# Graph network of four layers on one core: the maximum's products in four row groups, the output projection in two banks

## What is computed

```python
# layer 0: normalised graph convolution, batch norm over all graphs, relu, + res_weight * h
# layer 1: attention over 8 heads of 32
scores = einsum('bhnd,bhmd->bhnm', Q, K) / sqrt(32)
attn = softmax(where(adj == 0, -inf, scores))
out = einsum('bhnm,bhmd->bhnd', attn, V) @ Wo.T + bo
# layer 2: (eps * x + adj @ x) @ W1 + b1, rms norm, silu, @ W2 + b2   (hidden width 1024)
# layer 3: attention of 4 heads with scores leaky_relu(e_i + e_j), masked, softmax, @ h
```

## Time and profile before

| | |
|---|---|
| median of 3 executions | 3992.91 us |
| lowest and highest | 3992.35 and 9107.89 us |
| profiled execution: span | 3982.8 us, the only time shown of it |
| PE busy | 3709.5 us (93%) |
| DVE busy | 3101.9 us (78%) |
| ACT, POOL busy | 1994.8 us (50%), 1576.2 us (40%) |
| mean granted TensorE clock | 0.953 |

### The profile page before, as it was taken

One profiled execution on the slowest core, in us unless ns is written; L12 is line 12 of the kernel. 1 busy time (PEld: TensorE's weight loads), 2 busy tenths in 40 slices (PEclk: granted clock), 3 DMA queues, 4 the chain that ended last, 5 costly groups with the idle time before them and its releaser, 6 DMA issues.

```text
span 3982.8 us, 59433 instructions
## 1 busy us (share of the span) xinstructions
PE 3709.5 (93%) x19042; PEld 2707.6 (68%) x19042; DVE 3101.9 (78%) x5637; ACT 1994.8 (50%) x3047; POOL 1576.2 (40%) x980
## 2 busy tenths in 40 slices
PE   7999579999999999999999999999999999999986
PEld 6888346676667766666666676766677666666665
DVE  6787557888887888888888888888878888888752
ACT  4656145555555555555545545555555555555430
POOL 4667234333443444444433333334434444444310
PEclk9999689999999999999999999999999999999986
DMA  8988322222222212222222222222222212222200
GB/s 286 317 310 298 93 53 64 70 69 69 63 58 69 60 52 56 53 69 69 69 69 69 69 69 69 69 69 63 58 69 59 58 52 53 69 69 69 53 16 11
DMA packets 195935, 341.10 MB, mean 86 GB/s; under 512 B 28720, under 2 KB 64432, under 8 KB 195888
## 3 DMA queue, kind: packets, MB, share of 16 engines
q1 hardware_dynamic: 195888, 340.50, 30.3%
HBM read 188.89 MB, written 50.33 MB: 60 GB/s over the span
## 4 chain that ended last, share of the span: by engine, by line
PE 78%; DVE 10%; ACT 4%; issue 3%; POOL 2%; DMA 2%; SPq 1%; DVEq 0%; ACTq 0%; POOLq 0%
PE bank L1444 12%; PE bank L1495 12%; PE obank L1378 12%; PE bank L1233 9%; PE pair L1233 7%; PE pair L1362 7%; PE bank L1406 6%; PE bank L1463 3%; PE pair L1339 3%; DVE minus_max L1033 2%; PE obank L1265 2%; DMA pT<-in_adjT 2%; PE bank L1265 1%; DVE b_st L841 1%; ACT hsq L632 1%
## 5 line engine op out<-in xcount | busy, mean ns | idle before, releaser
L602 POOL TENSOR_TENSOR pT<-pT,node_edge 128x1024 f32<-128x1024 f32 x256 | 628.6, 2462 | 532.0 <-ACT pT L690 530.1
L690 ACT ACTIVATE pT<-pair 128x1024 f32<-128x1024 f32 x512 | 515.9, 1031 | 325.6 <-PE obank L1378 248.2
L1033 DVE TENSOR_REDUCE minus_max<-pair 128x2 f32<-128x1024 f32 x512 | 603.3, 1216 | 56.9 <-PE pair L1339 56.5
L1023 DVE TENSOR_TENSOR pT<-pT,node_edge 128x1024 f32<-128x1024 f32 x256 | 399.8, 1562 | 269.4 <-ACT pT L690 266.2
L1495 PEld LDWEIGHTS bank<-v,p3T 128*128 128x128 f32 x4096 | 502.4, 199 | 36.2 <-DVE p3T L1182 24.5
L1495 PE MATMUL bank<-v,p3T 128*128 128x65 f32 x4096 | 499.8, 280 | 20.2 <-DVE p3T L1182 20.2
L540 POOL TENSOR_TENSOR d_rs<-d_ve,minus_half 128x4 f32<-128x4 f32 x32 | 32.2, 1007 | 1207.5 <-DVE d_ve L853 1207.5
L1378 PE MATMUL obank<-pT,v 128*64 128x512 f32 x2048 | 490.3, 611 | 8.4 <-POOL pT L602 4.8
L1444 PE MATMUL bank<-w_s,hid 128*128 128x256 f32 x2048 | 479.6, 389 | 0.3 <-DVE hid L1112 0.3
L1444 PEld LDWEIGHTS bank<-w_s,hid 128*128 128x128 f32 x2048 | 383.6, 192 | 87.7 <-issue 40.1
L632 ACT ACTIVATE p3T<-x,d_sh,d_rs 128x256 f32<-128x256 f32 x128 | 66.4, 589 | 720.6 <-POOL d_sh L546 720.6
(11 more groups left out here) (189 smaller groups left out, 6468.7 us busy)
## 6 DMA issues: line engine op xcount, KB each, us to landing
pT<-in_adjT SPq DMA_DIRECT2D x64, 512.0 KB, 5.3
a_at<-in_adjT SPq DMA_DIRECT2D x64, 512.0 KB, 3.6
q_parts<-high_parts SPq DMA_DIRECT2D x256, 128.0 KB, 4.7
k_parts<-high_parts SPq DMA_DIRECT2D x256, 128.0 KB, 4.1
b_at<-in_adjT SPq DMA_DIRECT2D x64, 512.0 KB, 3.9
hid<-in_x SPq DMA_DIRECT2D x32, 512.0 KB, 4.4
x_res<-hid SPq DMA_DIRECT2D x32, 512.0 KB, 5.0
pre_bn<-hsq SPq DMA_DIRECT2D x32, 512.0 KB, 4.1
```

What stands on the lines that cost most here:

```text
L602: nc.gpsimd.tensor_tensor(half, half, node_edge[:, 0:2, :], ALU.mult).then_inc(a_masked[0].sem, 1)
L690: nc.scalar.activation(dst, pair[p][:, :, :], func, **more).then_inc(a_copied[p].sem, 1)
L1023: nc.vector.tensor_tensor(half, half, node_edge[:, 2:4, :], ALU.mult).then_inc(a_masked[1].sem, 1)
L1033: nc.vector.tensor_reduce(minus_max[:, t, 2 * two_heads:2 * two_heads + 2], pair[p][:, :, :], AX.X, ALU.max, negate=True).then_inc(a_copie ...
```

## The change

- `a_nat` does two former steps at once: for one node block and four heads, four matmuls in four row groups (0, 32, 64, 96) into both pairs, after a wait for both. There are 8 such steps. They stand in `ORDER` where the first or the second of the two steps stood; `a_max` keeps its 16 steps and their places and follows the new layout.
- The output projection goes to `bank[0]` and `bank[1]` (V_WO); the waits of DVE, POOL and `b_ln` follow. The two banks have 8 fills a graph for 7.
- `minus_max` is wider, set to zero once, and is transposed with 128 columns.
- `put_shift` issues one DMA for 8.
- The sorting is split: the high parts wait for the high parts alone (and the last scores), the low parts for the low ones. Number and order of its DMAs stay.
- The remaining steps of `ORDER` keep their order. A scratch size of the builder is set to 1024.

The diff, cut to its core:

```diff
@@ -16,8 +16,8 @@
 A_FILLS = 18
-O_FILLS = 1 + H1 // 2 + 2
-B_FILLS = (7, 7, 6 + 2 * H3)
+O_FILLS = 1 + H1 // 2
+B_FILLS = (8, 8, 6 + 2 * H3)
 RING = 4
@@ -77,16 +77,15 @@
-b.sumsq4:2 b.tanh0:3 p.v1:0 h.values31:3 b.tanh1:3 a.load0:0 a.nat00:0 a.nat01:0 b.out20:2 a.nat10:0 a.headc3:2
-a.vmask1:1 p.qhigh:1 a.nat11:0 b.tanh2:3 b.out21:2 h.prob0:3 a.vmask2:1 h.head0:3 a.nat20:0 a.nat21:0 b.out22:2
...
-b.flip31:2 a.div0:1 b.diag:2 a.nat61:0 b.e:2 a.vmask6:1 a.nat70:0 b.sumsq7:2 b.scale0:2 b.scale1:2 a.vmask7:1
...
+b.sumsq4:2 b.tanh0:3 p.v1:0 h.values31:3 b.tanh1:3 a.load0:0 a.nat0:0 b.out20:2 a.nat1:0 a.headc3:2 a.vmask1:1
+p.qhigh:1 b.tanh2:3 b.out21:2 h.prob0:3 a.vmask2:1 h.head0:3 a.nat2:0 b.out22:2 a.nat3:0 a.vmask3:1 b.out23:2 a.wo0:1
+a.nat4:0 b.tanh3:3 p.khigh:1 h.prob1:3 a.wo1:1 a.vmask4:1 a.nat5:0 h.head1:3 p.vc:1 b.norm3:3 b.ms:2 a.vmask5:1
+b.flip30:2 b.sumsq5:2 a.nat6:0 h.prob2:3 b.sumsq6:2 b.flip31:2 a.div0:1 b.diag:2 b.e:2 a.vmask6:1 a.nat7:0 b.sumsq7:2
...
@@ -163,7 +162,7 @@
         node_edge = sb("node_edge", P, T, N, dt=bf16)
-        minus_max = sb("minus_max", P, T, H1)
+        minus_max = sb("minus_max", P, (T - 1) * H1 + P)
         row_buf = sb("row_buf", P, N)
@@ -279,10 +278,9 @@
         a_qk_in = signal("a_qk_in", 24, 16)
-        a_shift_in = signal("a_shift_in", H1, 16)
+        a_shift_in = signal("a_shift_in", 1, 16)
         a_filled = [signal(f"a_filled{i}", A_FILLS) for i in range(2)]
         a_copied = [signal(f"a_copied{i}", A_FILLS) for i in range(2)]
-        wo_sum = signal("wo_sum", 2)
         shift_sum = signal("shift_sum")
@@ -321,7 +319,7 @@
         U_HT, U_Q, U_K, U_V, U_NAT, U_ST = 0, 1, 2, 3, 4, 20
-        V_AGG, V_HID, V_MS, V_RB, V_OUT, V_HT, V_E, V_VT, V_V3, V_HEAD = 0, 2, 10, 11, 12, 14, 16, 17, 18, 20
+        V_WO, V_AGG, V_HID, V_MS, V_RB, V_OUT, V_HT, V_E, V_VT, V_V3, V_HEAD = 0, 2, 4, 12, 13, 14, 16, 18, 19, 20, 22
@@ -481,28 +479,41 @@
-            def sort_parts(u, dst, srcs):
+            def sort_high(i, dst, src, places):
+
+                def f(g):
+                    r = DH1
+                    sp.wait_ge(*a_high_ok.upto(g, i + 1))
+                    if not first(g):
+
+                        for p in range(2):
+                            sp.wait_ge(*a_filled[p].upto(g.plus(-1), A_FILLS))
+                    for c in places:
+                        for n in range(P // r):
+                            sp.dma_start(dst[c * r:(c + 1) * r, n::P // r, :].bitcast(f32),
+                                         src[n * r:(n + 1) * r].bitcast(f32)).then_inc(a_qk_in.sem, 16)
+                return f
+
+            def sort_low(u, dst, src, c):
...
                     sp.wait_ge(*a_copied[p].upto(g, n + 1))
-                    for c, src in enumerate(srcs):
-                        for i in range(P // r):
-                            sp.dma_start(dst[c * r:(c + 1) * r, i::P // r, :].bitcast(f32),
-                                         src[i * r:(i + 1) * r]).then_inc(a_qk_in.sem, 16)
+                    for n in range(P // r):
+                        sp.dma_start(dst[c * r:(c + 1) * r, n::P // r, :].bitcast(f32),
+                                     src[n * r:(n + 1) * r]).then_inc(a_qk_in.sem, 16)
                 return f
...
                 sp.wait_ge(*o_copied.upto(g, 1))
-                for h in range(H1):
-                    sp.dma_start(q_parts[ROW_SHIFT:ROW_SHIFT + 1, h, :].bitcast(f32),
-                                 shiftT[h:h + 1, :].bitcast(f32)).then_inc(a_shift_in.sem, 16)
+                sp.dma_start(q_parts[ROW_SHIFT:ROW_SHIFT + 1, :, :].bitcast(f32),
+                             shiftT[:, :].bitcast(f32)).then_inc(a_shift_in.sem, 16)
...
                 "a.load": load_a, **{f"a.load{q}": load_at(q) for q in range(2)}, "b.load": load_b,
-                "p.sortq": sort_parts(U_Q, q_parts, (q_high.bitcast(f32), q_high.bitcast(f32), q_low)),
-                "p.sortk": sort_parts(U_K, k_parts, (k_high.bitcast(f32), k_low, k_high.bitcast(f32))),
+                "p.sortqh": sort_high(0, q_parts, q_high, (0, 1)), "p.sortql": sort_low(U_Q, q_parts, q_low, 2),
+                "p.sortkh": sort_high(1, k_parts, k_high, (0, 2)), "p.sortkl": sort_low(U_K, k_parts, k_low, 1),
                 "a.putshift": put_shift, "h.store": store})
@@ -527,14 +538,15 @@
                     nc.gpsimd.memset(u_parts[:, :].bitcast(f32), 0.0).then_inc(late.sem, 1)
-                    pool.wait_ge(late.sem, 4)
+                    nc.gpsimd.memset(minus_max[:, :], 0.0).then_inc(late.sem, 1)
@@ -577,7 +589,8 @@
-                    pool.wait_ge(*o_copied.upto(g, 0))
+                    for p in range(2):
+                        pool.wait_ge(*b_copied[p].upto(g.plus(-1), 1))
                 nc.gpsimd.tensor_tensor(a_xbo[:, :, :], a_o[:, :, :], bo_s[:, None, :].broadcast_to([P, T, D]),
@@ -1023,14 +1036,15 @@
-            def a_max(h, q):
-                two_heads, t = divmod(2 * h + q, T)
-
-                def f(g):
-
-                    p, n = a_unit(U_NAT + 2 * h + q)
+            def a_max(j, p):
+                chunk, t = divmod(j, T)
+                two_heads = 2 * chunk + p
+
+                def f(g):
+
+                    _, n = a_unit(U_NAT + 2 * j + p)
                     dve.wait_ge(*a_filled[p].upto(g, n + 1))
-                    nc.vector.tensor_reduce(minus_max[:, t, 2 * two_heads:2 * two_heads + 2], pair[p][:, :, :], AX.X, ALU.max,
+                    nc.vector.tensor_reduce(minus_max[:, t * H1 + 2 * two_heads:t * H1 + 2 * two_heads + 2], pair[p][:, :, :], AX.X, ALU.max,
                                             negate=True).then_inc(a_copied[p].sem, 1)
@@ -1049,19 +1063,22 @@
                 def f(g):
-                    dve.wait_ge(*wo_sum.upto(g, q + 1))
+                    bank_, n = b_unit(V_WO + q)
+                    dve.wait_ge(*b_filled[bank_].upto(g, n + 1))
                     dve.wait_ge(*a_xbo_ok.upto(g, 1))
...
                     half = slice(2 * q, 2 * q + 2)
-                    nc.vector.tensor_tensor(x_mid[:, half, :], obank[:, :].rearrange("p (b d) -> p b d", d=D),
-                                            a_xbo[:, half, :], ALU.add).then_inc(o_copied.sem, 1)
+                    nc.vector.tensor_tensor(x_mid[:, half, :], bank[bank_][:, :].rearrange("p (b d) -> p b d", d=D),
+                                            a_xbo[:, half, :], ALU.add).then_inc(b_copied[bank_].sem, 1)
                 return f
...
             def b_ln(g):
-                dve.wait_ge(*o_copied.upto(g, O_FILLS))
+                for q in range(2):
+                    p, n = b_unit(V_WO + q)
+                    dve.wait_ge(*b_copied[p].upto(g, n + 1))
                 stats("b", g, x_mid)
@@ -1327,18 +1344,19 @@
-            def a_nat(h, q):
-                two_heads, t = divmod(2 * h + q, T)
+            def a_nat(j):
+                chunk, t = divmod(j, T)
...
                     pe.wait_ge(*a_high_ok.upto(g, 2))
-                    dst, full = a_free(g, U_NAT + 2 * h + q)
-                    for b in range(2):
-                        chunk, r = divmod((2 * two_heads + b) * DH1, P)
-                        i = nc.tensor.matmul(dst[:, b, :], q_high[r:r + DH1, chunk, t * P:(t + 1) * P],
-                                             k_high[r:r + DH1, chunk, :], start=True, stop=True)
-                    i.then_inc(full, 1)
+                    into = [a_free(g, U_NAT + 2 * j + p) for p in range(2)]
+                    for p, (dst, full) in enumerate(into):
+                        for b in range(2):
+                            r = (2 * p + b) * DH1
+                            i = nc.tensor.matmul(dst[:, b, :], q_high[r:r + DH1, chunk, t * P:(t + 1) * P],
+                                                 k_high[r:r + DH1, chunk, :], start=True, stop=True)
+                        i.then_inc(full, 1)
                 return f
@@ -1348,14 +1366,14 @@
                 for t in range(T):
-                    i = nc.tensor.transpose(obank[0:H1, t * P:(t + 1) * P], minus_max[:, t, :], ident[:, :])
+                    i = nc.tensor.transpose(obank[:, t * P:(t + 1) * P], minus_max[:, t * H1:t * H1 + P], ident[:, :])
                 i.then_inc(shift_sum.sem, 1)
...
                     pe.wait_ge(*a_qk_in.upto(g, 24))
-                    pe.wait_ge(*a_shift_in.upto(g, H1))
+                    pe.wait_ge(*a_shift_in.upto(g, 1))
                     dst, full = a_free(g, U_ST + 2 * h + q)
@@ -1385,12 +1403,12 @@
                         pe.wait_ge(*a_divided.upto(g, K))
-                    pe.wait_ge(*o_copied.upto(g, O_FILLS - 2 + q))
+                    dst, full = b_free(g, V_WO + q)
                     for t in (2 * q, 2 * q + 1):
                         for k in range(K):
-                            i = nc.tensor.matmul(obank[:, (t % 2) * D:(t % 2 + 1) * D], att1T[:, k, t * P:(t + 1) * P],
+                            i = nc.tensor.matmul(dst[:, (t % 2) * D:(t % 2 + 1) * D], att1T[:, k, t * P:(t + 1) * P],
```

(36 more changed lines are left out.)

## The result

| | before | after |
|---|---|---|
| median | 3993.81 us | 4021.05 us (4020.68 to 4021.26, 4 runs) |
| ratio | 1 | 1.0067, 95% interval 1.0054 to 1.008 |
| profiled span | 3982.8 us | 4019.4 us |
| mean granted clock | 0.953 | 0.939 |

The kernel became 0.7% slower, 27 us; the interval leaves out 1. The forecast was 3982 us, a little faster; the measured time lies inside the range of 3940 to 4050, on the other side.

What follows compares the result with a forecast made beforehand. Bounds: DVE from x3's second half to the shift, PE elsewhere, and the granted clock. Terms -0.46 + 0.1, say -0.35 us, over 32 graphs: -11; span 3972, with 10.1 added 3982 us; range 3940 to 4050.

Steps and rivals of the forecast that it cites:

- Who sets the path: DVE is the path from x3's second half to the shift transposes (2658.40 to 2676.85); elsewhere PE is.
- The x_mid wait of 1.48 us: PE's wait before the output projection's second half: two banks remove it, worth 0 at full clock, bounds 0 and 1.48.
- Four groups, PE's cost: Maximum's products: four matmuls in four row groups take 0.44 us of PE instead of 0.66.
- The gain up to the projection: Maximum steps 0 to 3, among the third-stage products: x3's second half starts 0.46 us earlier.
- Step 2 waits for its maxima: Maximum step 2 on PE starts about 2649.5 as today, so the first two steps' gains turn into waiting.
- Step 5 late by 0.1: Maximum step 5 waits for the maximum ahead of x_mid's second half; its banks fill late, costing DVE 0.1 us.
- Wide transposes, one transfer, sorting at nothing: 128-column shift transposes (cost 0.01 us), one row DMA for eight and split sorting: value 0.
- The clock's share kept at 1.2 us: Loss per graph to the clock falling from 2.4 to 1.2 GHz: between 0 and about 2.3, kept at 1.2.
- since one cause goes and another comes: Reason for keeping 1.2 us: idle before the projection goes, about 2 us each before steps 5 and 6 comes.
- The slow rival: Clock falls at steps 5 to 7 in every graph, slowing key product and aggregation: +3.4 us, 4052 us; chance 0.15.
- Its price of 3.4: Half rate's cost per graph in that rival: 1.7 us for the key product plus 1.7 for the aggregation.
- the 10.1 us between span and median: Shown median 3992.9 us less profiled span, added to the forecast span of 3972 to give 3982 us.

Runs made afterwards that it cites:

- e6: Kernel before with only the output projection in two banks, plus 15 unused products of constants on PE: 3961.23 us, ratio 0.9922.
- e1: Changed kernel plus 17 unused products of constants on PE, ahead of maximum steps 5, 6, 7 and the key product: 3960.16 us, ratio 0.9918.
- e10: Changed kernel plus unused products of constants only ahead of maximum steps 5 and 6, six each: 3960.86 us, ratio 0.992.
- e4: Kernel before with only wide transposes, one row transfer instead of eight and split sorting: 3992.16 us, ratio 0.9997.
- e3: Kernel before with only the output projection in two banks, maximum's products two at a time: 3986.2 us, ratio 0.9983.
- e5: Changed kernel with maximum steps 5, 6 and 7 again as two halves, each waiting for one pair: 3971.08 us, ratio 0.9945.
- e9: Changed kernel with PE and DVE reordered from step 5 to the shift, unused products added, two waits its trace showed removed: 3904.42 us, ratio 0.9779.
- e7: Changed kernel with PE and DVE reordered from step 5 to the shift, DVE's x_mid statistics first, no filler: 4007.12 us, ratio 1.0036.

## Why the prediction was wrong

- **Who sets the path: right at full clock.** There it is DVE from x3's second half to the shift. The x_mid wait of 1.48 us vanished and came back ahead of step 5 as 2.12; e6 shows that it was worth nothing at full clock. At half rate the path leaves DVE for PE, from step 6 to the end of the key product.
- **Four groups, PE's cost: right.** 0.44 us, as taken. The gain up to the projection was 0.46 by the forecast and is 0.44: from the first of these products to the projection the kernel before took 2658.10 - 2640.87 = 17.23, and it is now 2683.47 - 2666.68 = 16.79. Step 2 waits for its maxima (0.47) as forecast.
- **Step 5 late by 0.1: nearly.** x_mid's second half to the next maxima took 2664.85 - 2664.25 = 0.60 and now takes 2690.38 - 2689.62 = 0.76: 0.16. With 0.04 more for a wide transpose the full-clock graph is 0.2 us shorter (104.46 in e1 and e10 for 104.67), not 0.35.
- **Wide transposes, one transfer, sorting at nothing: right** (e4, 0.9997). The drain that the Trainium skill ("TensorEngine Tiling (Array Packing)", "Key Properties") puts at a change of mode shows no price here: the shift's four take 2704.99 - 2704.52 = 0.47 us with 128 columns and took 0.43 with 8. That 8 columns are another mode at all was my reading; no run shows it.
- **The clock's share kept at 1.2 us: the step that failed.** It was the term of the sum with bounds 0 and about 2.3, and I set it in the middle "since one cause goes and another comes". Measured, it is 106.53 - 104.47 = 2.1 us, and that reason failed twice. What was to go did not go: with the x_mid wait gone and nothing else changed (e3), the key product is at half rate in every graph, for 9 of 20 before, and that still costs 0.8. And what came was larger, for I had put at nothing that the double wait of step 6 makes the key product start later. I let a slow key product cost up to 1.7. In the graph shown it ends 1.80 later for its own length (3.78 for 1.98 in e1) and 0.74 later for its start (5.79 for 5.05, step 6 and the second transpose being slow too), less 0.45 that DVE had to spare: 2.1. e5, which takes the double waits of steps 5 to 7 away and leaves the half rate, gives 104.84.
- **The slow rival.** Its mechanism, half rate over the key product in every graph, is what happened, and I had given it a chance of 0.15. Its price of 3.4 was too high: the aggregation, which it charged with 1.7, is not on the path. Its own 4052 us lay just outside my range.
- **A side error.** I took the 10.1 us between span and median for what lies around the span. That is 4021.18 - 4019.4 = 1.8 us; the other 8 are that the profiled execution of the kernel before was quicker than its median. It does no harm, since 3982.8 + 10.1 is the median shown, and 3982 is that median less 11.

## What to carry to other kernels

Where another engine is the path, making TensorE's work there shorter and its waits fewer but longer can cost time: TensorE may run its next long product at half rate, and a step that waits for more makes that product start later. Here half rate with an early start cost 0.8 us a graph (e3), the late start at full clock nothing (e1, e10), and both together 2.1. Before merging small steps, list the idle time that each wait leaves, what runs behind it, and how much the other engine has to spare before it needs that result. Where a PSUM bank is free, products of constants in those gaps, short enough to end before the awaited data come, kept the clock at 1.00 and turned a loss of 0.7% into a gain of 0.8%. With another order on top it was 2.2% (e9); the other order without filler was 0.4% slower than the kernel before (e7).

## What was not expected of the hardware

- Twelve products without use, six in each of two gaps of 2 us, kept the clock at its upper level through all 20 graphs, and their exact number and place mattered little: e1 with 17 and e10 with 12 give 104.47 and 104.46 us, and e6 with 15 in shorter gaps holds it too.
- The fall needs no long idle time: the longest wait of PE in the changed kernel's loop is listed as 2.1 us, and in e3, where the key product is at half rate in every graph, those ahead of it were 0.7 us and less.
- A lower mean clock is not a slower kernel: e3 and e5 have 0.946 and 0.947 and beat the kernel before with 0.953. What counts is whether another engine waits for the product in the slow stretch.
